# A one-core ViT block: who clears the hidden tile, and the order and pieces of the first loads

## The reference, cut to what matters

```python
p = layernorm(patches(x), ln1_g, ln1_b)              # 1152 x 768
h = layernorm(p @ W_proj, ln2_g, ln2_b)              # 1152 x 192
h = layernorm_plain(h + attention(h))                # over channels, 8 heads of 24
h = layernorm_plain(h + soft_moe(h))                 # 8 experts, 4 slots each, hidden 24
```

## Time and profile before

| | us |
|---|---|
| median of 3 runs | 115.49 |
| lowest, highest | 115.33, 116.55 |
| the profiled execution, its own time | 115.89 |
| its span (first to last instruction) | 114.1 |

### The profile page before, as it was taken

The page is one execution under the profiler, slowest core; times in us unless marked ns, Lnnn a source line. Parts: engine busy times, 40 slices in busy tenths (PEclk is TensorE's granted clock), DMA queues, the critical chain, the costliest instruction groups (busy, mean ns, idle before and its releaser), DMA issues.

```text
span 114.1 us, 4793 instructions
## 1 busy us (share of the span) xinstructions
PE 102.0 (89%) x1775; PEld 89.5 (78%) x1775; DVE 89.6 (79%) x380; ACT 62.6 (55%) x211; POOL 53.1 (47%) x125
## 2 busy tenths in 40 slices
PE   6899989999999996999989695999999979999910
PEld 6799979989898985898878685889877858988600
DVE  0529576866999769969658797999998897999960
ACT  4000023619194937595773756698867795459370
POOL 8800542489865884913608332120330331067780
PEclk9999999999999999999999999999999999999985
DMA  3999997985931001011000431100000000001332
GB/s 86 245 341 406 352 382 163 331 313 129 331 109 37 1 0 38 0 35 35 6 3 9 97 90 35 40 0 11 0 6 0 6 0 3 0 6 50 96 100 65
DMA packets 8554, 11.28 MB, mean 99 GB/s; under 512 B 2357, under 2 KB 5877, under 8 KB 8533
## 3 DMA queue, kind: packets, MB, share of 16 engines
q1 hardware_dynamic: 8533, 11.00, 30.6%
HBM read 9.22 MB, written 0.88 MB: 89 GB/s over the span
## 4 chain that ended last, share of the span: by engine, by line
PE 60%; DVE 15%; issue 9%; POOL 7%; ACT 3%; DMA 2%; POOLq 1%; SPq 0%; DVEq 0%
PE ps L477 7%; PE ps L565 5%; PE ps L505 5%; PE ps L556 5%; PE ps L508 4%; PE ps L661 4%; PE ps L503 3%; PE ps L590 3%; PE ps L542 3%; PE ps L631 3%; PE ps L529 3%; PE ps L488 2%; DMA gb<-in_ln_gb 2%; PE ps L576 2%; PE ps L456 2%
## 5 line engine op out<-in xcount | busy, mean ns | idle before, releaser
L477 PE MATMUL ps<-wc,xT 128*128 128x192 f32 x108 | 18.7, 327 | 0.0
L477 PEld LDWEIGHTS ps<-wc,xT 128*128 128x128 f32 x108 | 17.5, 190 | 0.1
L1043 ACT ACTIVATE hT<-ps,b,g 128x128 f32<-128x128 f32 x18 | 7.3, 465 | 16.7 <-PE ps L488 16.7
L1243 POOL TENSOR_SCALAR mv<-mv 108x1 f32<-108x1 f32 (+1 forms) x11 | 2.8, 251 | 21.1 <-DVE mv L853 21.0
L1065 ACT ACTIVATE km<-ps,imgsel 108x192 f32<-108x192 f32 (+1 forms) x32 | 11.1, 421 | 2.4 <-PE ps L512 2.4
L1054 ACT ACTIVATE sq<-ps 108x384 f32<-108x384 f32 (+1 forms) x11 | 5.5, 500 | 7.8 <-PE ps L512 7.7
L661 PE MATMUL ps<-wu,hb 128*96 128x192 f32 (+1 forms) x44 | 8.8, 330 | 0.5 <-DVE hb L932 0.4
L565 PE MATMUL ps<-wp,yT 128*108 128x192 f32 (+1 forms) x44 | 9.2, 332 | 0.0
L723 DVE BATCH_NORM_STATS2 st<-xs 128x6 f32<-128x384 f32 x18 | 9.0, 542 | 0.0
L505 PE MATMUL ps<-wqk,hT 128*108 128x192 f32 (+1 forms) x44 | 9.0, 326 | 0.0
L1248 POOL TENSOR_TENSOR r<-mv,halves 108x2 f32<-108x2 f32 (+1 forms) x11 | 8.2, 747 | 0.5
(11 more groups left out here) (116 smaller groups left out, 300.4 us busy)
## 6 DMA issues: line engine op xcount, KB each, us to landing
xs<-in_x SPq DMA_DIRECT2D x9, 384.0 KB, 7.1
xT<-in_x_t SPq DMA_DIRECT2D x9, 384.0 KB, 7.1
out<-o SPq DMA_DIRECT2D x10, 81.0 KB
wt<-in_w_tok SPq DMA_DIRECT2D x2, 288.0 KB, 3.4
wqk<-in_w_qk SPq DMA_DIRECT2D x1, 192.0 KB, 5.5
wp<-in_w_proj SPq DMA_DIRECT2D x1, 192.0 KB, 11.1
wd<-in_w_down SPq DMA_DIRECT2D x1, 192.0 KB
z<-h SPq DMA_DIRECT2D x2, 81.0 KB
```

Of the source, the lines that this page charges most:

```text
L477: mm = pe.matmul(tokp(t), xT[:, o + kc * 128:o + (kc + 1) * 128], wc[:, kc, :], start=kc == 0, stop=kc == KC - 1)
L1043: ins = act.activation(hT[:, f, t * 128:(t + 1) * 128], htp(t)[:, f, :], ACT.Identity, bias=b2[:, f:f + 1], scale=g2[:, f:f + 1])
```

## The change

- GpSimd no longer clears hb. ScalarE does it at the head of its list with one activation (Copy with scale 0.0, reading a column of `still`, writing 2048 values per partition), and signals a semaphore of its own. The count of the shared semaphore falls from 6 to 5 for all its waiters.
- norm1 is issued ahead of the token weights.
- The token weights come in 3 transfers of 192 KB instead of 2 of 288 KB. column_means waits for each as it gets there.
- xT(0) is issued ahead of x(0), xT(1) ahead of x(1), and xT(2) ahead of x(2) as before, with x(1) between xT(1) and xT(2).
- 5 constant products instead of 6.

```diff
+WP = 3
-        wtok_in = [sem(f"wtok_in{i}") for i in range(2)]
+        wtok_in = [sem(f"wtok_in{i}") for i in range(WP)]
+        hb_cleared = sem("hb_cleared")
             def load_token_weights(i):
-                k0 = i * KC // 2
-                sp.dma_start(wt[:, k0:k0 + KC // 2, :].rearrange("p k e -> p (k e)"),
-                             w_tok[:, k0 * D:(k0 + KC // 2) * D]).then_inc(wtok_in[i], 16)
+                k0 = i * KC // WP
+                sp.dma_start(wt[:, k0:k0 + KC // WP, :].rearrange("p k e -> p (k e)"),
+                             w_tok[:, k0 * D:(k0 + KC // WP) * D]).then_inc(wtok_in[i], 16)
-            load_token_weights(0); load_norm1(); load_token_weights(1); load_x(0); load_turned(0)
-            load_x(1); load_turned(1); load_turned(2); load_x(2); load_turned(3); load_ident()
+            load_norm1(); load_token_weights(0); load_token_weights(1); load_token_weights(2); load_turned(0)
+            load_x(0); load_turned(1); load_x(1); load_turned(2); load_x(2); load_turned(3); load_ident()
-                for _ in range(6):
+                for _ in range(5):
                     pe.matmul(ps[:, 2, 0:D], still[:, 0:128], still[:, :], start=True, stop=True)
-                    if kc % (KC // 2) == 0:
-                        pe.wait_ge(wtok_in[kc // (KC // 2)], 16)
+                    if kc % (KC // WP) == 0:
+                        pe.wait_ge(wtok_in[kc // (KC // WP)], 16)
-                    dve.wait_ge(cleared, 6)
+                    dve.wait_ge(hb_cleared, 1)
+            def clear_hidden():
+                act.wait_ge(still_ready, 1)
+                act.activation(hb[:, :, :, :, :].rearrange("p e i n q -> p (e i n q)"),
+                               still[:, 0:1].broadcast_to([128, 2 * B * NE * NP]), ACT.Copy,
+                               scale=0.0).then_inc(hb_cleared, 1)
-            take_h(0); take_h(1); take_qk(0); take_v(0); square(0); norm_logs(0); take_h(2)
+            clear_hidden(); take_h(0); take_h(1); take_qk(0); take_v(0); square(0); norm_logs(0); take_h(2)
-            pool.memset(hb[:, :, :, :, :], 0.0).then_inc(cleared, 1)
-            pool.wait_ge(cleared, 6)
+            pool.wait_ge(cleared, 5)
```

More of the change, by code:

```diff
@@ L413, in load_experts @@
                 sp.dma_start(bu[:, :], b_up).then_inc(experts_in, 16)
-                sp.wait_ge(cleared, 6)
+                sp.wait_ge(cleared, 5)
                 for j in range(4):
@@ L461, in offset @@
                 pe.wait_ge(ln1_in, 16)
-                pe.wait_ge(wtok_in[0], 16)
-                pe.wait_ge(wtok_in[1], 16)
+                for i in range(WP):
+                    pe.wait_ge(wtok_in[i], 16)
                 for kc in range(KC):
@@ L1050, in square @@
                 if g == 0:
-                    act.wait_ge(cleared, 6)
+                    act.wait_ge(cleared, 5)
                 if g >= 2:
```

## The result

The changed kernel takes 116.61 us (median of 22 runs), the kernel before, run beside it, 115.89 (22 runs). The ratio is 1.0062 with a 95% interval of 1.0034 to 1.0089: slower by 0.7 us. The profiled execution of after has a span of 114.9 us against 114.1.

What follows compares the result with a forecast made beforehand. TensorE is bound by its opening chain and, at turn_h(2), by bprow's landing. -0.85 (column_means) +0.40 (x(1)) +0.45 (wait for bprow) +0.2 (bprow later) = +0.2 on 115.89: 116.1, or 115.7 for the median; range 114.6 to 116.5.

Steps and rivals of the forecast that it cites:

- What bounds the opening: Before column_means: GpSimd's memset of hb holds up VectorE's gs1, which takes 1.66 us on 6 values per partition.
- The gate: At turn_h(2): the arm from bprow through row_sum meets TensorE's list, so 0.45 us won earlier are spent waiting.
- I take 0.2 later: Landing of bprow in the DMA queue: 0.2 us later, as the first large transfer starts 0.47 later, partly made up.
- The bound of 0.47: Landing of bprow: at most 0.47 us later, if the whole step of one more transfer shows up.
- the pieces move the same bytes: Token weights in 3 parts: the split leaves the bytes in the queue ahead of bprow the same.
- What was won in the opening: column_means runs from 4.45 to about 6.8 instead of to 7.68, winning 0.85 us; x(1) leaves 0.45.
- Kept distances: Everything behind turn_h(2) keeps its distances, as GpSimd's and VectorE's lists also hang on row_sum.
- a tie of 0.17 us: At turn_h(2): TensorE's own list arrives with only 0.17 us to spare against the arm from bprow.
- Rival 3: DMA queue: smaller pieces and later head cost more than 0.47 us; at 0.6 later, 116.1 us; chance 0.12.
- Rival 1: At row_sum: bprow is no gate, TensorE's arm decides; 115.0, or 114.6 with x(1) early too; chance 0.18.
- Rival 2: TensorE's clock stays at its lower level through column_means, price 1.75 us; about 116.3 us; chance 0.07.
- the gap that I had named: Before column_means: TensorE stands still if weights part 0 lands after 4.42, keeping the clock low; forecast landing 4.0.

Runs made afterwards that it cites:

- clear_five: Kernel before with hb cleared by ScalarE and 5 constant products, all transfers as before; ratio 0.9952.
- before_same: The kernel before itself, unchanged, run again for a second look at bprow's landing; 115.45 us.
- before_same2: The kernel before itself, unchanged, a third look at bprow's landing; 115.93 us.
- before_turned: Kernel before with only the order of the big tiles changed: xT(0), x(0), xT(1), x(1), xT(2), x(2); ratio 0.9956.
- after_again: The changed kernel once more, unchanged, as a second look at its landings; ratio to the kernel before 0.9973.
- before_split: Kernel before with the token weights in 3 parts, norm1 still behind the first, nothing else; ratio 1.0033.
- before_split2: Kernel before with the token weights in 3 parts and nothing else, a second look; 115.59 us.
- after_xold: Changed kernel with x(0), xT(0), x(1), xT(1), xT(2), x(2) in their old order; ratio to the kernel before 0.9987.
- after_row: Changed kernel with row_sum moved behind ln1_root(4) in GpSimd's list; ratio to the kernel before 0.9958.
- best: Kernel before with hb cleared by ScalarE, 5 products, row_sum behind ln1_root(4), norm1 first, weights in 2 parts, old x and xT order; ratio 0.9894.
- after_two: Changed kernel with the token weights in 2 parts of 288 KB again; ratio to the kernel before 0.9982.

## Why the prediction was right and where it was wrong

**What bounds the opening: right.** The memset of hb held gs1: without it gs1 took 0.35 us in after, 0.17 in clear_five. gb landed at 2.5, 0.7 us earlier than the forecast had it, which changed nothing: gs1 was ready before the constant products ended, as said. ScalarE's clearing took 1.91 us between 2.0 and 3.9 (bounds 0.5 to 2.7) and cost nothing.

**The gate: right.** That what is won ahead of 22 us is spent in front of bprow was the step on which the forecast rested. In the 13 profiles in which TensorE (its products or its weight load) waits for VectorE at turn_h(2) with row_sum in its old place, row_sum's start is followed by turn_h(2) after 2.91 to 2.92 us; in the other three (before_same, before_same2, before_turned) the distance is 2.98 to 3.49. The wait for bprow grew from 1.0 to 1.6 us in after and turn_h(2) waited 0.52, as predicted, but this is luck. The forecast had GpSimd come to row_sum 0.45 us earlier and bprow 0.2 later; GpSimd came 0.71 later and bprow 1.22 later, and the difference happens to be as large.

**"I take 0.2 later" for bprow: the step that failed.** It was 1.22 in the profile of after and 0.25 in that of after_again, against the earlier trace rows; the mean of the two, 23.0, is 1.0 later than the mean of the three profiles of before, 22.0. The bound of 0.47 rested on "SyncE issues every later transfer 0.47 us later", and on a later issue costing nothing where the queue is full. Both failed. The step of 0.47, read from the first issues, holds only up to about 4 us; bprow was issued 1.15 us later in after and 0.97 in after_again, and in after it took the same 10.0 us from there to its landing as in the earlier trace rows. With the split bprow is issued 0.7 us later on the mean and lands 0.6 to 0.7 later. I took "the pieces move the same bytes" to mean that they cost the same. The Trainium skill, "DMA: Bandwidth & Descriptors", section "Rules for kernel authors", asks for fewer and larger transfers; the landings in before_split and before_split2 agree with its direction. The issue times speak for the number of the pieces rather than their size, but no run has one more issue without smaller pieces.

**What was won in the opening.** The forecast put 0.85 us at column_means. It was 0.65 in after, as part 2 of the weights landed at 6.0, my upper bound, and the product that needs it stood still. x_stats(1) was to wait until 10.7 for x(1) and waited until 11.88, so turn_h(0) came at 16.65 instead of 15.5. The forecast had x(1) land where xT(1) did before, at 10.6, and it landed at 11.8: 0.47 us of that is the later issue (4.01 against 3.54), which I put at nothing, and 0.7 more the time from issue to landing (7.8 against 7.1). With the tiles in their old order, in after_xold, turn_h(0) starts at 15.35.

**In the sum** the terms read -0.65 at column_means, then +1.36 up to turn_h(0) (0.71 late), and +0.51 from there to turn_h(2), together the 1.22 us by which turn_h(2) is late. TensorE's own arm, 25.88 in place of 24.7, would have made it 0.7 late even with bprow as early as before; bprow added the rest. What lies behind gave 0.4 back. From turn_h(2) to the end it is 88.5 us here, 88.9 in before, and 87.7 to 88.9 in the others of the 13, so this part scatters and isn't the change's.

**Kept distances.** The kernel before isn't always held by bprow. In its two further profiles row_sum starts at 21.95 and 21.78, and turn_h(2) at 25.44 and 25.11, more than 2.92 behind: TensorE's arm is the last. I read a tie of 0.17 us in one trace as the rule. It is one draw: the landing moves by up to 1 us and TensorE's opening by some tenths, and the end takes the later of the two. A later landing costs only what exceeds TensorE's arm.

**The rivals.** Rival 3, the transfers come later, is what happened. Its price, each microsecond at bprow one at the end, was too high: bprow landed at 23.36, at the mark of 23.35 set for 1%, and the kernel was slower by 0.6%. Rival 1 would have needed a free gate; it needed an edit, row_sum moved. Rival 2, the clock, is there in some executions. Instructions of column_means in after, and in after_row (ns, min/median/max):

```profile
L458 PE MATMUL ps<-wt,gs x12: 326/326/429, 4.2 to 6.7; 128*128 128x192 f32 x12
```

```profile
L458 PE MATMUL ps<-wt,gs x12: 326/524/524, 4.5 to 7.6; 128*128 128x192 f32 x12
```

In after_row most records of column_means run at the lower level (524 ns against 326, though the granted clock reads 1.00 in both, as in the opening of before), and it takes 3.46 us instead of 2.23. In after_again it takes 3.31, in best 3.07. TensorE did not stand still before it in these three, so not the gap that I had named brought it about. With 6 products it took 2.55 at most (before_same). Whether the sixth product protects, or three of nine profiles against none of eleven is chance, is not settled. The Trainium skill, "TensorE: Matmul & The Clock Gate", section "Part 1: The HAM clock gate (the "warmup" mystery)", says that the number of slow products varies between runs of one kernel; after and after_again, the same program with 2.8 and 3.3 us for column_means (the first with its stop inside), agree.

**What stays open.** The first comparison says 1.0062 (1.0034 to 1.0089), the later one of the same kernel 0.9973 (0.9928 to 1.0017). They don't agree. The later ratio rests on 6 executions, and the median of all 12 is 116.54 against 115.89 for the kernel before, which would be 1.006 again. So the cost of 0.7 us stands on the first comparison; the second neither confirms nor refutes it. The scatter of the landing, 1 us in one kernel, is of the size to do it, but that wasn't measured run by run. And it isn't settled why after_two lands late.

## What to carry to other kernels

Before a gain is counted, look down every list for the next wait on a transfer and ask how far from it the gaining arm is: a tiny load (here a row of 192 numbers) deep in a full DMA queue can set the end for three engines, because other engines' work stands behind it in one list. Put the instruction that waits for it behind the work that doesn't need it; that one move went with 0.4% here (0.9956, up to 0.9994) before anything else was changed, and with it the gain of the opening reached turn_h(2). And count transfers, not only bytes: one more at the head of the list went with an issue 0.7 us later for a transfer 20 places behind, more than the step of 0.47 at the head. When a landing comes late, look first whether it was issued late.

## What the runs showed of the hardware

- A GpSimd memset of 2048 values per partition stretched a VectorE operation on 6 values from 0.17 us (clear_five) to 1.66 (before). The operation ended 0.03 us after the memset. Issued with gb ahead of the weights, before that memset began, it took 0.32 to 0.52.
- An activation that writes 2048 values per partition takes 1.91 us, 0.93 ns for each value, where 384 values took 501 ns, 1.3 ns each.
- The landing of one and the same transfer, with the same program, differed by 1 us between two executions (after and after_again), 0.2 of it in the issue and 0.7 from issue to landing, though everything ahead of it in the queue was the same.
- SyncE's issues were 0.47 us apart up to 3.5 us (before) and 4.5 us (after); behind that single issues took up to 1.38 us (x(2) in after) while nothing in the list made them wait for another engine.
- Three transfers in place of two at the head of the queue, of the same bytes, went with a landing 1.1 to 1.2 us later for a transfer 20 places behind (before_split and before_split2, against three profiles of before). Over 19 profiles its issue was 0.67 us later with three.
